# Layer 0 attention: the causal mask of every second score step added by VectorE instead of TensorE

## The reference

```python
c_kv = x @ W_DKV                                  # latent, 64 wide
k = (c_kv @ W_UK).reshape(b, t, h, hd)
v = (c_kv @ W_UV).reshape(b, t, h, hd)
q = (x @ W_UQ).reshape(b, t, h, hd)
scores = jnp.einsum('bqhd,bkhd->bhqk', q, k) * scale
scores = jnp.where(causal, scores, -jnp.inf)
probs = jax.nn.softmax(scores, axis=-1)
ctx = jnp.einsum('bhqk,bkhd->bqhd', probs, v).reshape(b, t, d)
return ctx @ W_O
```

## Time and profile before

| | |
|---|---|
| median of 3 runs | 2090.08 us (2089.43 to 2093.64) |
| the profiled execution | 2090.87 us |
| its span | 2089.0 us |
| mean granted TensorE clock | 0.931 |
| PE busy over the span | 1777.4 us (85%) |
| DVE busy | 1168.1 us (56%) |
| ACT busy | 1057.0 us (51%) |
| POOL busy | 984.3 us (47%) |

### The profile page before, as it was taken

How to read it: one execution, slowest core, us unless ns; L and a number is a source line. 1 busy time by engine, 2 the same in 40 slices (tenths; PEclk the granted TensorE clock), 3 DMA queues, 4 the chain that set the end, 5 groups by cost and what they waited for, 6 DMA issues and landing times. The chain is left out here.

```text
span 2089.0 us, 34151 instructions
## 1 busy us (share of the span) xinstructions
PE 1777.4 (85%) x11015; PEld 1144.5 (55%) x11015; DVE 1168.1 (56%) x2538; ACT 1057.0 (51%) x1439; POOL 984.3 (47%) x736
## 2 busy tenths in 40 slices
PE   4888898887999999999997848878878888866999
PEld 2455555544878788788785623334334334334566
DVE  5666666562243353353442348877877877926535
ACT  1555555555422232232222117877877877963542
POOL 3344444432333434334333317776776776954202
PEclk7999999997999999999998958989989989988999
DMA  3333333315411120111110173232222222107346
GB/s 109 93 102 101 97 91 101 86 47 177 143 61 33 45 78 23 55 53 43 60 43 24 34 258 87 62 77 85 61 73 89 61 71 81 32 11 289 100 150 212
DMA packets 119221, 182.52 MB, mean 87 GB/s; under 512 B 14197, under 2 KB 73077, under 8 KB 119146
## 3 DMA queue, kind: packets, MB, share of 16 engines
q1 hardware_dynamic: 109214, 170.45, 27.1%
q10 hardware_dynamic: 9296, 9.05, 1.3%
q0 software_dynamic: 640, 2.10, 0.3%
HBM read 90.72 MB, written 39.91 MB: 63 GB/s over the span
## 5 line engine op out<-in xcount | busy, mean ns | idle before, releaser
L803 POOL TENSOR_TENSOR l_prob<-l_prob,l_bias 128x1024 f32<-128x1024 f32 x192 | 452.2, 2377 | 148.4 <-ACT l_prob L918 147.6
L1202 POOL TENSOR_TENSOR f_hl<-f_full,f_hh 128x512 fp32r<-128x512 f32 x192 | 247.6, 1290 | 425.6 <-DVE f_hh L1240 271.2
L985 DVE CUSTOM_DVE_ANT_0 l_slot<-l_slot,l_bias 128x512 f32<-128x512 f32 x512 | 340.8, 716 | 52.0 <-PE l_slot L1063 51.0
L921 ACT ACTIVATE l_prob<-l_prob 128x1024 f32<-128x1024 f32 x256 | 271.1, 1071 | 0.0
L472 DVE TENSOR_REDUCE l_peak<-l_slot 128x2 f32<-128x256 f32 (+3 forms) x256 | 206.4, 822 | 108.1 <-PE l_slot L564 105.8
L1288 PE MATMUL f_ps<-f_hh,f_hi_h 128*128 128x512 f32 x1024 | 259.9, 391 | 0.8 <-ACT f_attn L1168 0.4
L1288 PE MATMUL f_ps<-f_hl,f_hi_h 128*128 128x512 f32 x1024 | 258.4, 390 | 0.0
L388 ACT ACTIVATE l_prob<-l_slot 128x1024 f32<-128x1024 f32 (+3 forms) x256 | 174.8, 706 | 101.7 <-PE l_slot L583 99.3
L1288 PEld LDWEIGHTS f_ps<-f_hh,f_hi_h 128*128 128x128 f32 x1024 | 192.3, 188 | 43.3 <-ACT f_hh L1214 2.1
L1288 PEld LDWEIGHTS f_ps<-f_hl,f_hi_h 128*128 128x128 f32 x1024 | 192.4, 188 | 39.7
L918 ACT COPY l_prob<-l_slot 128x1024 f32<-128x1024 f32 x192 | 194.8, 1014 | 36.6 <-PE l_slot L1079 35.8
(11 more groups left out here) (205 smaller groups left out, 2844.4 us busy)
## 6 DMA issues: line engine op xcount, KB each, us to landing
l_stacks<-l_parts SPq DMA_DIRECT2D x384, 128.0 KB, 2.6
attn<-l_out_sb ACTq DMA_DIRECT2D x16, 512.0 KB, 2.9
f_raw<-in_L_ffn_h_w SPq DMA_DIRECT2D x16, 512.0 KB, 3.8
f_raw<-in_L_ffn_h_w SPq DMA_DIRECT2D x32, 256.0 KB, 2.6
e_w<-in_L_ffn_f SPq DMA_DIRECT2D x32, 256.0 KB, 2.9
l_bias<-ext SPq DMA_DIRECT2D x16, 448.0 KB, 6.4
l_x_in<-in_L_attn_x SPq DMA_DIRECT2D x8, 512.0 KB, 3.9
xh<-l_xh SPq DMA_DIRECT2D x8, 512.0 KB, 2.6
```

Source lines behind the costliest of these rows:

```text
L803: return eng.tensor_tensor(probs(n), src, bias[:, h:h + 2, j * P:j * P + T], ALU.add)
L921: act.activation(probs(n), probs(n), ACT.Exp).then_inc(p_exp.sem, 1)
L985: ins = dve.tensor_tensor_reduce(src, src, bias[:, 4 * g + 2 * pr + a, t * P:t * P + T], 1.0, 3 * NEG, ALU.add, ALU.max, peak[:, g, a, pr, ...
L1202: pool.tensor_tensor(t.hl[layer % 2][:, o], t.full[:, n % 2], t.hh[layer % 2][:, o].bitcast(F32), ALU.subtract).then_inc(self.h_lo.sem, 1)
```

## The change

In the steps with n % 4 = 0 or 2, the even ones, TensorE leaves out its four mask matmuls, and the second score matmul signals `a_ps`. VectorE adds a 128 x 128 fp32 mask, broadcast over the two heads, onto the diagonal part of the tile in PSUM, in place, signals a new semaphore `a_masked`, waits for it, and reduces as before. In the odd steps nothing changes. The mask comes by one more DMA at the start, on SP ahead of the v and output weights, and everybody who waited for the masks waits for three loads.

```diff
--- before.py
+++ after.py
@@ -112,6 +112,7 @@
         STEPS, LAG, RING = 32, 13, 4
 
         ident, cols, power = sb("ident", [P, P]), sb("cols", [P, 4]), sb("power", [P, TT])
+        mask = sb("mask", [P, P])
         half, half_b = sb("half", [P, 2, 2, P]), sb("half_b", [P, 2, 2, P], BF16)
         c_low = cols[:, 3:4]
 
@@ -160,6 +161,7 @@
         stack_in = [sem(f"stack_in{g}", 6, unit=16) for g in range(QUADS)]
         tops_in = [sem(f"tops_in{g}", 2, unit=16) for g in range(QUADS)]
         a_ps, a_max = sem("a_ps", STEPS), sem("a_max", STEPS)
+        a_masked = sem("a_masked", STEPS // 2)
         m_ps, tops_ready = sem("m_ps", QUADS), sem("tops_ready", QUADS)
         b_ps, p_exp, p_done = sem("b_ps", STEPS), sem("p_exp", STEPS), sem("p_done", STEPS)
         value_ps, o_copied, ot_ps = sem("value_ps", QUADS * TT), sem("o_copied", QUADS), sem("ot_ps", 2)
@@ -254,6 +256,10 @@
             g, pr, t = n // 8, n // 4 % 2, (0, 3, 1, 2)[n % 4]
             return g, pr, t, max((t + 1) * P, MIN_N)
 
+        def by_dve(n):
+
+            return n % 4 in (0, 2)
+
         def prob_of(n):
 
             g, j, pr = n // 8, n // 2 % 4, n % 2
@@ -299,7 +305,7 @@
                 for name in ("c", "q", "k"):
                     for dst, src in w["place"](name, raw[name], dict(w["loads"])[name]):
                         sp.dma_start(dst, src).then_inc(w_in[name].sem, 16)
-                for dst, src in ((cols, c["c_cols"]), (half, c["c_half"])):
+                for dst, src in ((cols, c["c_cols"]), (half, c["c_half"]), (mask, c["c_mask"][:, T - P:T])):
                     sp.dma_start(dst[:], src).then_inc(masks_in.sem, 16)
                 for dst, src in w["place"]("v", raw["v"], dict(w["loads"])["v"]):
                     sp.dma_start(dst, src).then_inc(w_in["v"].sem, 16)
@@ -352,7 +358,7 @@
                 rounded(wq[:, 0], raw["q"][:])
                 act.wait_ge(w_in["k"].sem, 16 * 2)
                 rounded(wk[:, 0], raw["k"][:, 0], HD ** -0.5)
-                act.wait_ge(masks_in.sem, 16 * 2)
+                act.wait_ge(masks_in.sem, 16 * 3)
                 act.copy(half_b[:], half[:]).then_inc(half_ready.sem, 1)
 
                 def more_high_weights():
@@ -452,7 +458,7 @@
                         dve.tensor_copy(xh[:], x_full[:]).then_inc(xh_ready.sem, 1)
                     if kind == "latent_low":
                         if opening(b):
-                            dve.wait_ge(masks_in.sem, 16 * 2)
+                            dve.wait_ge(masks_in.sem, 16 * 3)
                         wait(dve, c_top, 1, b)
                         dve.scalar_tensor_tensor(cs[:], top[:].bitcast(F32), c_low, m_bank[:],
                                                  ALU.mult, ALU.add).then_inc(c_ready.sem, 1)
@@ -469,6 +475,11 @@
                     if kind == "score":
                         g, pr, t, wide = score_of(n)
                         wait(dve, a_ps, n + 1, b)
+                        if by_dve(n):
+                            diag = slot(kind, n)[:, :, t * P:(t + 1) * P]
+                            dve.tensor_tensor(diag, diag, mask[:].unsqueeze(1).to_broadcast([P, 2, P]), ALU.add)\
+                               .then_inc(a_masked.sem, 1)
+                            wait(dve, a_masked, n // 2 + 1, b)
                         dve.tensor_reduce(peak[:, g, :, pr, t], slot(kind, n)[:, :, 0:(t + 1) * P], AX_X, ALU.max)\
                            .then_inc(a_max.sem, 1)
                     if kind == "maxima":
@@ -556,9 +567,10 @@
                         diag = slice(t * P, (t + 1) * P)
                         for a in range(2):
                             r = head(a, HROWS - 1)
-                            pe.matmul(out[:, a, 0:wide], stacks[r, 0, 2 * g + pr, diag], stacks[r, 1, 2 * g + pr, 0:wide],
-                                      start=True, stop=False, skip_group_check=True)
-                        for part in range(2):
+                            ins = pe.matmul(out[:, a, 0:wide], stacks[r, 0, 2 * g + pr, diag],
+                                            stacks[r, 1, 2 * g + pr, 0:wide],
+                                            start=True, stop=by_dve(n), skip_group_check=True)
+                        for part in () if by_dve(n) else range(2):
                             for a in range(2):
                                 r, first = head(a), part * HROWS
                                 ins = pe.matmul(out[:, a, t * P + first:(t + 1) * P], half_b[r, part, 0],
```

## The result

The changed kernel took **2102.64 us** (median of 4 runs, 2099.92 to 2104.01); the kernel before, beside it, 2089.76 (4 runs, 2086.01 to 2093.64). The ratio is 1.006, 95% interval 1.0044 to 1.0077. It is slower by 12.9 us, where 6.5 were forecast: the direction came as forecast, the size is twice it, inside the range.

A forecast was written before the change was run, and what follows sets the result against it. It took VectorE as full from the reduction of step 1 to the x transpose, with a TensorE chain on even steps. Its terms, +6.7 + 2.0 - 2.2 = +6.5 us, gave a median of 2096.6, range 2089 to 2105.

The forecast's parts named there:

- Term 1: Reduction of step 1 to x transpose: five VectorE adds, less gaps, cost +0.96 per stretch, +6.7 us over 7.
- Term 2: Output projection of step 24 waits for the reduction of step 22, which ends later: +0.28, 7 times, +2.0 us.
- Term 3: TensorE without even-step masks: 0.10 saved per place, kept in steps 0, 16 and 24, about 22 places, -2.2 us.
- count nothing: Other even steps: P or a later S waits for the exponential or VectorE, so no TensorE saving was counted.
- The clock: Rival: looped batches' stretches to the x transpose mostly run at the slower clock; all seven +6.7 us, 2103; chance 0.12.
- TensorE's chain wins: Rival: VectorE's gaps take the adds, every even step keeps TensorE's saving, 2066 to 2077 us; chance 0.11.
- Both effects meet: Rival: layernorm-stretch cost half as large, through earlier statistics or score, about +1.4 us, 2091.5; chance 0.20.

The follow-up runs named there:

- e2: Changed kernel, but VectorE adds the mask only in steps 2, 4, 6, 8 and 10, TensorE in all others: 2102.04 us, ratio 1.0049.
- e7: Changed kernel, but VectorE adds the mask in step 10 alone: 2090.48 us (one run).
- e8: Changed kernel, but VectorE adds the mask in step 2 alone: 2087.40 us (one run).
- e5: Changed kernel, but step 22 gets its mask from TensorE again: 2097.65 us, ratio 1.0051.
- e1: Changed kernel, but steps 2 to 10 get their mask from TensorE again; VectorE adds only in even steps 0 and 12 to 30: 2087.43 us, ratio 0.9989.
- e3: Changed kernel without VectorE's add, so nobody masks the score on even steps: 2083.57 us, ratio 0.9968.
- e4: Changed kernel with TensorE's mask matmuls back in all steps and VectorE's even-step adds kept: 2108.87 us, ratio 1.0092.
- e6: Kernel before, with no mask added to the score in any step; the causal select behind the exponential masks: 2081.73 us, ratio 0.9967.
- e9: The changed kernel, unaltered, profiled once more: 2102.66 us, ratio 1.0052.

## Why the prediction was right in direction and half in size

*Term 1, layernorm stretch: right.* Forecast +0.96 per stretch, measured 12.70 to 13.62, +0.92. Its parts held too: 0.46 per add, and VectorE with 13.38 of 13.62 us busy. e2 shows that these five adds are the loss. One part of its working was lax: I set five adds against all gaps of the stretch. e7 and e8 show that the place decides. It came out right because all four gaps lie behind the add of step 2, and the last of them, ahead of the reduction of step 9, still behind that of step 8; only step 10's add finds none.

*Term 2, the output projection: right.* Forecast +0.28; e5 shows 0.24 to 0.25 at clock 1.00. It was all but cancelled by TensorE's saving elsewhere, which the forecast missed: e1 carries this term, and its clean batch is 54.38 against 54.33.

*Term 3, TensorE's saving: right in the single place, too small in number.* 0.10 each, as V at 0.32 instead of 0.42 behind S shows, and at 0.22 instead of 0.31 where S stands directly behind P. The Trainium skill ("TensorE: Matmul & The Clock Gate", Part 3) has a weight load overlap only where its row group differs from that of the matmul in flight; by it V cannot follow S as soon as M did, and the trace agrees (0.32 against 0.23, and 0.22 against 0.12). I counted 22 places in the stage, about 3 per batch. e3 gives 0.8 per batch where VectorE pays nothing, that is 8 places, and the changed kernel against e4 0.7. The even steps at which I "count nothing" are the ones missed.

*The sum of the work.* Forecast per batch +0.96 + 0.28 - 0.31 = +0.93; measured 55.31 - 54.33 = +0.98. Two misses cancel in it: without any saving the adds cost 1.7 (e4), not 1.24, and the saving is 0.7, not 0.31. That the sum came out so near is luck. In batches 1 to 6 that is 5.9 us; the forecast has 5.6 for these six, and 6.5 for seven.

*The step that failed: the clock.* "The clock" stood only as a rival, with 0.12, for one stretch, and the sum held its cost at what before showed. Measured, the slower level took 7.0 us more in batches 1 to 6. None of it came from the stretch I had named, which is slow in one batch of six now (15.04 in batch 4; two in the second profile) and was in two before. Most of it came where TensorE is the bound: 24 full matmuls of the output projection that grow from 3.09 to 4.38 us, four batches of six. The full timeline of the changed kernel, batches 2 and 3:

```profile
190.30 4.38 PE L524 MATMUL l_slot<-l_wo,l_mixt 128*128 128x256 f32 x22 [0.27 <-DVE l_peak L483]
...
248.18 3.09 PE L524 MATMUL l_slot<-l_wo,l_mixt 128*128 128x256 f32 x24 [0.27 <-DVE l_peak L483]
```

(Two of the 24 records are missing in the first.) The rival's figure, 2103, is what was measured, but by another road: that is luck too.

The second share is batch 0, 2.7 us more. The rival took five stretches in the looped batches, where there are six, and batch 0's as one at clock 1.00. But its stretch runs at the 1.2 GHz level in both kernels, and there the adds cost 1.5 (14.30 and 14.49 to 15.96 and 15.90), not 0.96. The reason for the 1.5 is in the windows above: VectorE's busy time rose by 2.05 us (11.24 to 13.29), but its idle time fell by only 0.39 (3.06 to 2.67), while at clock 1.00 it fell by 0.85 (12.74 - 11.65 to 13.62 - 13.38): the waits for a slower TensorE stay. The other 1.2 us of batch 0 I did not trace. Against both shares stand the 3.4 us by which batch 7 and the rest of the stage are shorter; the forecast had nothing on them.

The Trainium skill (same page, Part 1) calls the throttled clock the default, which activity releases. That pointed to the dearer side, and the time came out there. But fewer matmuls alone brought little of it (e3: 8.7 over clean, e6: 7.9, against 5.9 and 6.8 before), and all of them back did not cure it (e4: 13.8). The four dear kernels share three things: the five adds of steps 2 to 10, a first stretch of 13.6 us or more, and a clean batch of 55.0 us or more. The 0.92 us wait at the x transpose they share too, but e7 has it and pays no more than the cheap kernels. Which of the three lowers the clock is open: no run lengthens the batch without filling that stretch, or fills it without lengthening the batch. Where the level falls is open as well; it moves with small shifts (e5, e2, and from one batch to the next in e9).

*The rivals.* "TensorE's chain wins" fell: its condition, adds below 0.27 each in the stretch, was not met. "Both effects meet" fell as well: term 1 came whole, +0.92, and not half as large.

## What to carry to other kernels

Moving work off the engine that looks busiest pays only where the receiving engine has a gap behind the place where the work lands: cost each moved instruction at its place in the order, since one add of 0.46 us at the end of a full stretch cost all of it, and one at its head nothing. Where a profile shows stretches at both clock levels, count in the sum what each long matmul group would lose at the lower one. And ask first whether the work is needed there at all: leaving the mask out ahead of the maxima did more than any way of sharing it.

## What the runs showed of the hardware that I had not expected

- The slower clock is a cost of its own size that comes and goes with the schedule: 34.1 and 37.5 us of batches 1 to 6 at that level in the two profiles of the changed kernel, 20.5 and 17.1 before (the granted clocks of 0.95 and 0.97 above). Its price depends on where it falls: one fall cost 1.34 in the stretch that waits for VectorE and 1.52 to 1.61 on the output projection.
- An fp32 add of 256 elements in PSUM, with its result written back in place, takes 426 ns, about as much as a product of the same size that is read out of PSUM and written elsewhere (420 ns).
- A full-height weight load after half-height matmuls leaves about 0.10 us on TensorE, whatever the half-height matmuls were: V follows M by 0.19 where P follows it by 0.09, and S by 0.32 (0.22 where S stands directly behind P) where M follows it by 0.23 (0.12).
